# Two state-space layers: which states' drives GpSimd forms, and when ScalarE ends the sigmoid of u

## The chip, the cores and the metric

The kernel runs on one NeuronCore of a Trainium2 chip. The metric is device time in microseconds (us): the median of three executions is 6466.08 us (6462.25 to 6472.54). The engines are called PE (TensorE, the matmuls), PEld (its weight loads), DVE (VectorE), ACT (ScalarE), POOL (GpSimd) and SP (SyncE, which issues the DMAs). Each engine works through its own queue in order and waits on semaphores for the others.

## What is computed

The input `x` is (4, 128, 64, 64). Two state-space (Mamba) layers come first, then a layer that picks top blocks and one of attention at three scales. Only the first two are touched. For each of 256 sequences of 128 steps, with 128 inner channels and 16 states:

```python
u  = silu(causal_conv4(u) + conv_b)
dt = softplus(x_dbl[..., :DT_RANK] @ W_dt.T + b_dt)
def step(h, inp):                       # one time step, 16 states a channel
    u_t, dt_t, B_t, C_t = inp
    h = exp(dt_t[:, :, None] * A) * h + (dt_t * u_t)[:, :, None] * B_t[:, None, :]
    y = einsum('bds,bs->bd', h, C_t)
...
y = (y + u * Dp) * silu(z);  return y @ W_out.T
```

`exp(dt*A)` is called the decay, `dt*u*B` the drive.

## The kernel before, in words

`mamba_layer` runs twice. Its work is cut into 32 chunks of 8 sequences, so that every operand is 128 channels x 1024 (8 sequences x 128 steps). A chunk has 16 units, one for each state s. A unit is:

- the drive: for 11 states PE spreads row B over the partitions into PSUM (`pe_rows`, L441, "rows"), and DVE multiplies it by `dtu` there (`dve_drive`, L563). For the five states of `POOL_UNITS` a DMA brings the row of B, broadcast, and POOL multiplies it by `dtu` (`pool_drive`, L611). PE and DVE have no drive in such a unit.
- the decay: ACT's Exp (L533), into a `decay` buffer, or, for a state of `POOL_UNITS`, into the PSUM pair `b_ps[s % 2]` that PE does not fill in that unit.
- the scan on DVE (L577), which writes `state[s % 4]` and waits for PE's sum of state s-4.
- POOL's product of the state with row C (L617), and PE's sum of it into `y_ps` (L453, "sum"), which runs three units behind (`LAG`).

Beside that, each unit s carries a step of the preparation of the next chunk (`*_prep`), at a fixed place in each queue. What matters here:

- PE in unit s issues: rows of s (none for a state of `POOL_UNITS`), the sum of s-3, then its step of the preparation. The steps are: unit 0 the transposes ("turn", L402), units 1 and 2 the products with `w_u` (L412), unit 5 `w_bc` (L419), unit 7 `w_dt` (L425), unit 10 `w_z` (L430), unit 14 the output product of the chunk before (L465). The sum of state 0, in unit 3, has `diag` (L450, two matmuls on `u`) ahead of it, which waits for the gate.
- DVE in unit s issues: drive of s, then the gate `yz` in unit 2 (L582, waits for the sum of state 15), or its step of the preparation (u in unit 4, L542; bc in 6; the lost part in 10; z in 13) or the add in 15, then the scan of s.
- POOL in unit s issues: product of s-1, its step of the preparation (units 11, 12, 13: L594, L598, L604, the last one makes `dtu`), then the drive of s+2 if that is a state of `POOL_UNITS`.
- ACT in unit s issues: the decay of s, then its step of the preparation. The sigmoid of u is Exp (L479), Ln (L482) and Exp (L485).
- SP loads row C of s once the product of s-4 is done, then row B of s+2 if POOL forms that drive.

Below, "s4", "D4", "d4" and "p4" are the scan, DVE's drive, POOL's drive and POOL's product of state 4; a prime marks those of the neighbouring chunk. "Sum13" is PE's sum of state 13, "rows4" PE's rows for D4.

Of the kernel before, what the change touches and what calls it, by code (L numbers as in the profile page):

```python
# [27 lines left out]
def wait(eng, sem, value):  # L28

    if isinstance(value, int) and value <= 0:  # L30
        return
    eng.wait_ge(sem, value)
# [250 lines left out]
C_AT = 2 * BLOCK  # L283
GATE_AT, OUT_AT, ADD_AT = 2, 14, 15
LOAD_AT, C_WRITE_AT = 8, 11
POOL_UNITS = (2, 4, 6, 8, 10)
DVE_UNITS = tuple(s for s in range(S) if s not in POOL_UNITS)
B_ROWS, DRIVE_AHEAD, B_LOAD_AHEAD = 5, 2, 2


def mamba_layer(nc, sem, tag, X, C, M, scale_c, bias_c):
# [3 lines left out]
    with Memory(nc, tag) as m:  # L295
# [67 lines left out]
        def by_pool(c, s):  # L363

            return c * len(POOL_UNITS) + sum(1 for k in POOL_UNITS if k <= s)

        def b_slot(s):
            return POOL_UNITS.index(s)

# [63 lines left out]
        def pe_rows(pe, c, par, s):  # L433
            unit = c * S + s
            if s == 0:
                wait(pe, s_lo, c + 1)
            if s in POOL_UNITS:
                return
# [31 lines left out]
        def act_prep(act, n, par, k):  # L470
            if k == 1:
                wait(act, s_turn, n + 1)
                wait(act, s_pz, 2 * n)
                nc.scalar.activation(xt[:, :], prep_ps[:, 0:HALF], ACT.Identity, scale=scale_c[:, bass.ds(n, 1)],
                                     bias=bias_c[:, bass.ds(n, 1)]).then_inc(s_xt, 1)
            if k == 3:
                wait(act, s_pu, 2 * n + 2)
                wait(act, s_log1p, n)
                nc.scalar.activation(gu[:, :], prep_ps[:, :], ACT.Exp, scale=-1.0,  # L479
                                     bias=M["neg_conv_b"][:, 0:1]).then_inc(s_gu, 1)  # L480
                wait(act, s_gu, 3 * n + 1)
                nc.scalar.activation(gu[:, :], gu[:, :], ACT.Ln, bias=1.0).then_inc(s_gu, 1)  # L482
            if k == 4:
                wait(act, s_gu, 3 * n + 2)
                nc.scalar.activation(gu[:, :], gu[:, :], ACT.Exp, scale=-1.0).then_inc(s_gu, 1)  # L485
            if k == 5:
                wait(act, s_pbc, n + 1)
                wait(act, s_b, len(DVE_UNITS) * (n - 1))
                nc.scalar.activation(bc[:, par, :], prep_ps[:, :], ACT.Copy).then_inc(s_hi, 1)
                wait(act, s_cw, 16 * n)  # L490
                nc.scalar.activation(c_out[C_AT:C_AT + BLOCK, :], prep_ps[C_AT:C_AT + BLOCK, :],
                                     ACT.Copy).then_inc(s_cc, 1)
            if k == 8:
                wait(act, s_pdt, n + 1)
                wait(act, s_dtu, n - 1)
                wait(act, s_decay, S * (n - 1))
                nc.scalar.activation(dt[:, par, :], prep_ps[:, :], ACT.Relu, bias=M["b_dt"][:, 0:1]).then_inc(s_pos, 1)
                wait(act, s_pos, n + 1)
                nc.scalar.activation(prep_ps[:, :], prep_ps[:, :], ACT.Abs, bias=M["b_dt"][:, 0:1]).then_inc(s_abs, 1)
                wait(act, s_abs, 2 * n + 1)  # L500
                nc.scalar.activation(prep_ps[:, :], prep_ps[:, :], ACT.Exp, scale=-1.0).then_inc(s_abs, 1)
            if k == 9:
                wait(act, s_abs, 2 * n + 2)
                nc.scalar.activation(ln_e[:, :], prep_ps[:, :], ACT.Ln, bias=1.0).then_inc(s_ln, 1)
                wait(act, s_u, n + 1)
                nc.scalar.activation(gu[:, :], prep_ps[:, :], ACT.Identity, bias=1.0).then_inc(s_one, 1)
            if k == 11:
                wait(act, s_pz, 2 * n + 2)
                wait(act, s_sz, n)
                nc.scalar.activation(gz[:, :], prep_ps[:, :], ACT.Exp, scale=-1.0).then_inc(s_gz, 1)  # L510
                wait(act, s_gz, 3 * n + 1)
                nc.scalar.activation(gz[:, :], gz[:, :], ACT.Ln, bias=1.0).then_inc(s_gz, 1)
            if k == 12:
                wait(act, s_gz, 3 * n + 2)
                nc.scalar.activation(gz[:, :], gz[:, :], ACT.Exp, scale=-1.0).then_inc(s_gz, 1)

        def act_unit(act, c, par, s):
# [7 lines left out]
            seq = lambda a: by_t(a)[:, :, 1:T]  # L525
            if s in POOL_UNITS:
                wait(act, s_scan, unit + 1 - PAIRS)
# [29 lines left out]
        def dve_drive(dve, c, par, s):  # L557
            if s in POOL_UNITS:
                return
            if s == 0:  # L560
                wait(dve, s_dtu, c + 1)
            wait(dve, s_b, by_dve(c, s))
            nc.vector.tensor_tensor(b_ps[s % PAIRS][:, :], dtu[:, par, :], b_ps[s % PAIRS][:, :],  # L563
                                    ALU.mult).then_inc(s_drive, 1)
# [84 lines left out]
        def act_both(act, c, par, s, prep):  # L649
            act_unit(act, c, par, s)  # L650
            if prep:
                act_prep(act, c + 1, 1 - par, s)
# [35 lines left out]
        with nc.Block() as block:  # L688
# [24 lines left out]
            @block.scalar  # L713
            def _(act):
                act.preload_act_table_set(EXP_LN_TABLES)
                for k in range(S):
                    act_prep(act, 0, 0, k)
                run(act, act_both)
# [971 lines left out]
```

## Time and profile before

| | us |
|---|---|
| median of three executions | 6466.08 |
| the profiled execution | 6468.96 |
| its span, first to last instruction | 6467.1 |
| span of the two state-space layers (about) | 79 to 1937 and 2000 to 3857 |

The profile names, for each instruction or group of them, start, duration, engine, line, tiles out<-in and, in square brackets, how long its engine sat idle before it and who ended that. Durations of neighbours on one engine overlap a little, since a successor starts while the predecessor drains; so distances from start to start are used where an engine is busy. PEclk is the clock granted to TensorE as a share of full speed.

### The profile page before, as it was taken

The numbers are of one execution on the slowest core, as the hardware profiler recorded it, in microseconds if no ns is written. First come the engines' busy times: TensorE is split into PE (matmuls) and PEld (weight loads), VectorE is DVE, ScalarE is ACT, GpSimd is POOL, SyncE is SP. The second block draws the span as 40 slices with busy tenths as digits, with TensorE's granted clock in tenths as the row PEclk, the third lists the DMA queues.
The fourth block names the chain that finished last, engine by engine and source line by source line (L and its number), as shares of the span: only waits on it lengthen the run. The fifth ranks groups of instructions, "written<-read, shape, count | busy, mean of one in ns | idle before, by whom it ended". The sixth has DMA issues, their size and how long they took to land. (4 is left out here: it accounts for less than half of the span.)

```text
span 6467.1 us, 77508 instructions
## 1 busy us (share of the span) xinstructions
PE 5083.2 (79%) x22442; PEld 2639.5 (41%) x22442; DVE 4970.1 (77%) x6243; ACT 3277.4 (51%) x3626; POOL 4744.4 (73%) x2140
## 2 busy tenths in 40 slices
PE   3888888888874888888888866852559899898980
PEld 1343333333332333333333335311336566566650
DVE  5999999999996999999999984016465665655548
ACT  3555555555543555555555530001447677677760
POOL 3999999999994999999999970000337677676760
PEclk9999999999997999999999995875879999999995
DMA  3555555555552555555555540861569999999991
GB/s 124 202 198 201 199 200 203 203 202 199 203 176 97 200 202 205 202 200 200 200 199 204 203 147 22 343 239 27 97 123 186 179 173 186 164 185 185 184 185 52
DMA packets 1414964, 1148.54 MB, mean 178 GB/s; under 512 B 1211624, under 2 KB 1216832, under 8 KB 1406656
## 3 DMA queue, kind: packets, MB, share of 16 engines
q1 hardware_dynamic: 1414850, 1147.21, 62.3%
q8 instruction: 48, 0.79, 0.0%
q14 instruction: 66, 0.54, 0.0%
HBM read 812.29 MB, written 20.68 MB: 129 GB/s over the span
## 5 line engine op out<-in xcount | busy, mean ns | idle before, releaser
L617 POOL TENSOR_TENSOR l_state<-l_state,l_c_row 128x1024 f32<-128x1024 f32 x1024 | 2404.3, 2366 | 72.6 <-DVE l_state L577 69.0
L1389 POOL TENSOR_TENSOR l3s_el<-l3s_s_sb,l3s_eh 128x1024 f16<-128x1024 f32 (+2 forms) x584 | 1168.5, 2011 | 1217.1 <-ACT l3s_s_sb L1374 1205.7
L453 PE MATMUL l_y_ps<-l_state,ident 128*128 128x512 f32 x4096 | 1987.8, 611 | 49.0 <-POOL l_state L617 48.2
L577 DVE TENSOR_TENSOR_SCAN l_state<-l_decay,l_b_ps 128x1024 f32<-128x1024 f32 x704 | 1608.7, 2285 | 74.8 <-ACT l_decay L533 3.4
L1397 DVE TENSOR_SCALAR_CACHE_REDUCE l3s_s_sb<-l3s_s_ps 128x512 f32<-128x512 f32 (+1 forms) x1096 | 753.8, 689 | 621.9 <-PE l3s_s_ps L1333 603.2
L453 PEld LDWEIGHTS l_y_ps<-l_state,ident 128*128 128x128 f32 x4096 | 781.5, 195 | 870.2 <-issue 676.6
L1346 PE MATMUL l3s_o_ps<-l3s_vt,l3s_et 128*128 128x257 f16 x4368 | 879.5, 279 | 191.0 <-DMA l3s_et<-l3s_el 125.1
L1373 ACT ACTIVATE l3s_eh<-l3s_s_sb,l3s_shift 128x1024 f16<-128x1024 f32 (+2 forms) x584 | 634.5, 1087 | 535.4 <-DMA l3s_et<-l3s_el 423.0
L563 DVE TENSOR_TENSOR l_b_ps<-l_dtu,l_b_ps 128x1024 f32<-128x1024 f32 x704 | 850.4, 1208 | 30.2 <-PE l_b_ps L441 28.4
L441 PE MATMUL l_b_ps<-l_bc,mamba_pick 128*128 128x512 f32 x1408 | 575.1, 491 | 295.5 <-DVE l_state L577 285.6
L1348 PE MATMUL l3s_o_ps<-l3s_vt,l3s_et 128*128 128x129 f16 x4368 | 788.6, 224 | 0.0
L611 POOL TENSOR_TENSOR l_b_row<-l_b_row,l_dtu 128x1024 f32<-128x1024 f32 x320 | 756.2, 2363 | 0.2
L577 DVE TENSOR_TENSOR_SCAN l_state<-l_b_ps,l_b_row 128x1024 f32<-128x1024 f32 x320 | 729.4, 2279 | 5.1 <-POOL l_b_row L611 3.2
L1374 ACT ACTIVATE l3s_s_sb<-l3s_s_sb,l3s_shift 128x1024 f32<-128x1024 f32 (+2 forms) x584 | 629.8, 1078 | 0.0
L1346 PEld LDWEIGHTS l3s_o_ps<-l3s_vt,l3s_et 128*128 128x128 f16 x4368 | 435.0, 100 | 436.4 <-issue 204.6
L441 PEld LDWEIGHTS l_b_ps<-l_bc,mamba_pick 128*128 128x128 f32 x1408 | 230.6, 198 | 761.3 <-DVE l_state L577 583.8
L1331 PE MATMUL l3s_s_ps<-l3s_xh 128*128 128x512 f16 (+1 forms) x1096 | 426.9, 389 | 91.1 <-DVE l3s_xl L1310 69.4
L1348 PEld LDWEIGHTS l3s_o_ps<-l3s_vt,l3s_et 128*128 128x128 f16 x4368 | 435.3, 100 | 111.3 <-issue 6.6
L533 ACT ACTIVATE l_decay<-l_dt,l0m_A 128x1016 f32<-128x1016 f32 x352 | 393.0, 1134 | 141.2 <-POOL l_dt L598 99.1
L533 ACT ACTIVATE l_decay<-l_dt,l1m_A 128x1016 f32<-128x1016 f32 x352 | 393.0, 1134 | 140.4 <-POOL l_dt L598 99.6
L1332 PE MATMUL l3s_s_ps<-l3s_xl,l3s_xh 128*128 128x512 f16 (+1 forms) x1096 | 426.1, 389 | 0.0
L1333 PE MATMUL l3s_s_ps<-l3s_xh,l3s_xl 128*128 128x512 f16 (+1 forms) x1096 | 425.2, 388 | 0.0
(335 smaller groups left out, 5428.1 us busy)
## 6 DMA issues: line engine op xcount, KB each, us to landing
l_c_row<-l_c_rows SPq DMA_DIRECT2D x1024, 512.0 KB, 3.9
l_b_row<-l_c_rows SPq DMA_DIRECT2D x320, 512.0 KB, 4.9
l_ring_a<-in_L_conv_W SPq DMA_DIRECT2D x28, 1024.0 KB, 11.1
l2b_ring_b<-in_L_conv_W SPq DMA_DIRECT2D x26, 1024.0 KB, 11.3
l_xs<-X SPq DMA_DIRECT2D x64, 256.0 KB, 5.3
l_ring_a<-in_L_conv_W SPq DMA_DIRECT2D x14, 704.0 KB, 12.7
l2b_ring_b<-in_L_conv_W SPq DMA_DIRECT2D x13, 704.0 KB, 12.7
l_ring_a<-in_L_conv_W SPq DMA_DIRECT2D x14, 640.0 KB, 12.1
```

Of the source, the lines that this page charges most:

```text
L441: last = nc.tensor.matmul(b_ps[s % PAIRS][:, half(h)], C["pick"][:, s * P:(s + 1) * P], bc[:, par, half(h)], start=True, stop=True)
L453: last = nc.tensor.matmul(y_ps[:, half(h)], C["ident"][:, :], state[:, s % STATES, half(h)], start=False, stop=(s == S - 1))
L533: nc.scalar.activation(seq(to), seq(dt[:, par, :]), ACT.Exp, scale=M["A"][:, s:s + 1]).then_inc(s_decay, 1)
L563: nc.vector.tensor_tensor(b_ps[s % PAIRS][:, :], dtu[:, par, :], b_ps[s % PAIRS][:, :], ALU.mult).then_inc(s_drive, 1)
L577: nc.vector.tensor_tensor_scan(state[:, s % STATES, :], by, add, 0.0, ALU.mult, ALU.add).then_inc(s_scan, 1)
L611: nc.gpsimd.tensor_tensor(row, row, dtu[:, par, :], ALU.mult).then_inc(s_bdrive, 1)
L617: nc.gpsimd.tensor_tensor(state[:, s % STATES, :], state[:, s % STATES, :], c_row[:, s % C_ROWS, :], ALU.mult).then_inc(s_hc, 1)
L1346: high = lambda stop: nc.tensor.matmul(o_ps[par][:, 0:2 * P + 1], et[:, 0, slot, j, :], vt[:, mt, 0:2 * P + 1], start=(mt == 0), stop=stop)
L1348: lows = lambda: nc.tensor.matmul(o_ps[par][:, P:2 * P + 1], et[:, 1, slot, j, :], vt[:, mt, P:2 * P + 1], start=False, stop=False)
L1373: nc.scalar.activation(eh[:, part, off:off + EXPW], src, ACT.Exp, bias=shift[:, par:par + 1]).then_inc(s_eh, 1)
L1389: nc.gpsimd.tensor_tensor(el[:, part, off:off + EXPW], s_sb[:, par, j * EXPW:(j + 1) * EXPW], eh[:, part, off:off + EXPW], ALU.subtract).t ...
L1397: nc.vector.tensor_scalar(s_sb[:, par, kb * W:(kb + 1) * W], s_ps[(par * NB + kb) % SLOTS][:, 0:W], 0.0, None, ALU.add, ALU.max, accum_out ...
```

## The change

```diff
-POOL_UNITS = (2, 4, 6, 8, 10)
+POOL_UNITS = (3, 5, 7, 9, 11)
@@ act_prep
                 wait(act, s_gu, 3 * n + 1)
                 nc.scalar.activation(gu[:, :], gu[:, :], ACT.Ln, bias=1.0).then_inc(s_gu, 1)
-            if k == 4:
                 wait(act, s_gu, 3 * n + 2)
                 nc.scalar.activation(gu[:, :], gu[:, :], ACT.Exp, scale=-1.0).then_inc(s_gu, 1)
```

The number of drives on each engine stays at 11 and 5. PE and DVE get rows and drives in units 2, 4, 6, 8 and 10, and lose those of 3, 5, 7, 9 and 11. POOL's drives move one unit later (they are now issued in units 1, 3, 5, 7 and 9), and with them SP's loads of row B. ACT's decays of the odd states 3 to 11 go to PSUM, those of the even ones to the `decay` buffers. The third function for u is issued in unit 3, behind the Ln, and so ahead of the decay of state 4.

## Rows read from the trace of the kernel before

**Rows 1.** The page's part 1: busy us (share of the span) xinstructions.
```profile
PE 5083.2 (79%) x22442; PEld 2639.5 (41%) x22442; DVE 4970.1 (77%) x6243; ACT 3277.4 (51%) x3626; POOL 4744.4 (73%) x2140
```

**Rows 2.** Busy time in one window, 30 chunks of layer 0: span, engines, PEclk, DMA.
```profile
182.00:1882.00 1700.00, 1477.85 (x4129) 667.18 (x4128) 1644.74 (x990) 944.51 (x1049) 1670.87 (x720) 0.97 0.58 201
```

**Rows 3.** The gate L582 in windows of layers 0 and 1, then its waits in each.
```profile
L582 DVE TENSOR_TENSOR l_yz<-l_sz,l_y_ps x31: 1195/1195/1222, 182.2 to 1882.1; 128x1024 f32<-128x1024 f32 x31
...
  PE l_y_ps L453: 6.2, 6
...
L582 DVE TENSOR_TENSOR l_yz<-l_sz,l_y_ps x31: 1194/1195/1222, 2100.5 to 3801.4; 128x1024 f32<-128x1024 f32 x31
```

**Rows 4.** Waits of all DVE drives, L563: released by whom, us, times.
```profile
  PE l_b_ps L441: 28.4, 37
```

**Rows 5.** Timeline of DVE: start, duration, line, tiles; two stretches of layer 0.
```profile
1025.35 2.28 DVE L577 TENSOR_TENSOR_SCAN l_state<-l_decay,l_b_ps 128x1024 f32<-128x1024 f32 x1
...
1072.10 1.21 DVE L563 TENSOR_TENSOR l_b_ps<-l_dtu,l_b_ps 128x1024 f32<-128x1024 f32 x1
1073.22 1.21 DVE L555 TENSOR_TENSOR l_sz<-l_prep_ps,l_gz 128x1024 f32<-128x1024 f32 x1
...
1091.02 1.20 DVE L582 TENSOR_TENSOR l_yz<-l_sz,l_y_ps 128x1024 f32<-128x1024 f32 x1
1092.13 2.28 DVE L577 TENSOR_TENSOR_SCAN l_state<-l_b_ps,l_b_row 128x1024 f32<-128x1024 f32 x1
1094.33 1.21 DVE L563 TENSOR_TENSOR l_b_ps<-l_dtu,l_b_ps 128x1024 f32<-128x1024 f32 x1
1095.67 2.29 DVE L577 TENSOR_TENSOR_SCAN l_state<-l_decay,l_b_ps 128x1024 f32<-128x1024 f32 x1
1097.88 1.26 DVE L542 SCALAR_TENSOR_TENSOR l_u<-l_prep_ps,l0m_conv_b,l_gu 128x1024 f32<-128x1024 f32 x1
1099.05 2.28 DVE L577 TENSOR_TENSOR_SCAN l_state<-l_b_ps,l_b_row 128x1024 f32<-128x1024 f32 x1
```

**Rows 6.** Timeline of POOL: p15 after a wait; p13 and p14; d2; d4.
```profile
1027.70 2.36 POOL L617 TENSOR_TENSOR l_state<-l_state,l_c_row 128x1024 f32<-128x1024 f32 x1 [1.33 <-DVE l_state L577]
...
1078.82 4.67 POOL L617 TENSOR_TENSOR l_state<-l_state,l_c_row 128x1024 f32<-128x1024 f32 x2
...
1086.61 2.36 POOL L611 TENSOR_TENSOR l_b_row<-l_b_row,l_dtu 128x1024 f32<-128x1024 f32 x1
...
1093.57 2.37 POOL L611 TENSOR_TENSOR l_b_row<-l_b_row,l_dtu 128x1024 f32<-128x1024 f32 x1
```

**Rows 7.** Timeline of PE from sum13 to the first sum of the next chunk.
```profile
1081.24 1.98 PE L453 MATMUL l_y_ps<-l_state,ident 128*128 128x512 f32 x4 [0.28 <-POOL l_state L617]
1083.06 0.60 PE L402 MATMUL l_prep_ps<-ident,l_xs 128*128 128x128 f32 x4
1084.13 0.73 PE L441 MATMUL l_b_ps<-l_bc,mamba_pick 128*128 128x512 f32 x2 [0.47 <-DVE l_state L577]
1084.70 1.88 PE L453 MATMUL l_y_ps<-l_state,ident 128*128 128x512 f32 x4
1086.51 1.98 PE L412 MATMUL l_prep_ps<-l_xt,l0m_w_u 64*128 64x512 f32 x8
1088.42 1.98 PE L453 MATMUL l_y_ps<-l_state,ident 128*128 128x512 f32 x4
1090.34 1.95 PE L412 MATMUL l_prep_ps<-l_xt,l0m_w_u 64*128 64x504 f32 x8
1092.22 0.73 PE L441 MATMUL l_b_ps<-l_bc,mamba_pick 128*128 128x512 f32 x2
1092.79 1.88 PE L450 MATMUL l_y_ps<-l_u,l0m_diag_Dp 128*128 128x512 f32 x4
1094.51 3.60 PE L453 MATMUL l_y_ps<-l_state,ident 128*128 128x512 f32 x8
```

**Rows 8.** One window at the lower clock, inside sum13; columns as in rows 2.
```profile
342.70:346.10 3.40, 3.35 (x4) 1.24 (x5) 3.40 (x3) 0.00 (x0) 3.28 (x2) 0.54 0.41 164
```

## The prediction, made before the kernel was run

> **What bounds the kernel now.** The page comes first, for a summary only: no engine is busy over 80% of the whole [rows 1], since several stages with different limits are mixed there. The window over 30 chunks of layer 0 is what counts: in 1700 us DVE is busy 1645 and POOL 1671 [rows 2]. Both are nearly full, so a chunk can only get shorter if both get less to do or stand still less. The period of a chunk is read from the gate, once in each: (1882.1 - 182.2) / 30 = 56.66 us in layer 0 and (3801.4 - 2100.5) / 30 = 56.70 in layer 1 [rows 3], 56.68 in the mean.
>
> The timelines give the parts. A POOL operation takes 2.32 us from start to start: d2 to d4 has three in 6.96 [rows 6]. POOL has 16 products, 5 drives and 3 steps of preparation, 24 x 2.32 = 55.7. On DVE a scan is followed after 2.20 (1092.13 to 1094.33); a drive with its own scan right behind it, which reads what it wrote, keeps it off for 1.34 (1094.33 to 1095.67), but a drive with something else behind it only 1.12 (1072.10 to 1073.22) [rows 5]. Before, DVE's floor is 16 x 2.20 = 35.2, nine drives ahead of their scan 12.1, the drives of 13 and 15 with something between 2.2, and the six other operations (gate 1.11, u 1.17, z, bc, lost part, add) about 6.4: 55.9. So DVE sets the period, and the 0.8 above its floor is mostly waits for PE: 37 waits of drives for rows, 28.4 us in all [rows 4], and waits of the gate for the sum of state 15 [rows 3]. POOL stands still once in a chunk, for s15 [rows 6]. PE has slack, but see where: from sum13, which waits for p13 [rows 7], to rows3 it is busy almost without a hole, and rows3 at 1092.22 is done (0.73) 1.4 us before D3 at 1094.33 wants it [rows 5, 7].
>
> **The change, part by part.** (a) DVE's drives 2, 4, 6 and 10 now have the gate, u, bc and the lost part between them and their scan. Four times 1.34 - 1.12 = 0.22 makes 0.9 less: DVE's floor becomes 55.0. I take the row's value; the bound on the other side is zero. The Trainium skill (VectorE: DVE Perf Modes, "The DRAIN you can't avoid") says that in a chain of DVE operations the semaphore after each costs nothing extra; by that the floor would stay at 55.9. The two distances 1.34 and 1.12 for the same operation speak against it.
>
> (b) D11 goes, which had w_z of unit 10 right ahead of its rows. D12 has a scan more in front of it, but sum8 too. From the start of the lost part: PE takes w_z (about 1.06 at full clock), sum8 1.7, rows12 0.8, against s10, s11 and D12's turn at 5.5. It may wait by 0 to 0.4; what hides it is the slack found below.
>
> (c) POOL's order changes at the seam of the chunks. Before it was p15, d2, p0, p1, d4, p2: d2 filled the time until s0 was done. Now it is p15, p0, d3, p1, p2, d5, p3, p4. Products come earlier in POOL's queue than they did, and fewer operations lie between p4 and the next p13: p4, d7, p5, p6, d9, p7, p8, d11, p9, p10, L594, p11, L598, p12, L604, that is 15 before p13.
>
> (d) PE's order changes too, and this is what I expect to decide. rows2 now stands between w_u of unit 1 and sum15, and rows4 stands behind diag and sum0, where rows3 had stood ahead of both. The chain, by starts [rows 7]: sum13 to turn 1.82; turn 0.55 (it lasts 0.60, the overlap of neighbours is 0.05 to 0.1; its 0.47 of waiting for s15 should go, as DVE has more slack); rows1 0.57; sum14 1.81; w_u 1.91; rows2 0.57; sum15 1.92; w_u 1.88; diag 1.72; sum0 1.72; rows4 0.73 and 0.07 for the handover: 15.27 from sum13's start to D4. Then DVE: D4 to u 1.12, u to s4 1.17 [rows 5], s4's start to p4 2.35 (1025.35 to 1027.70) [rows 5, 6]. Then POOL: 15 x 2.32 = 34.8 to the next p13, and p13's start to sum13 2.42 (1078.82 to 1081.24) [rows 6, 7]. This is a closed circle through PE, DVE and POOL, and no queue can go around it faster: 15.27 + 4.64 + 34.80 + 2.42 = 57.13 us.
>
> A second circle goes through the gate. Sum13 to sum15's start 7.23, sum15 to the gate 2.05 (its duration 1.98 and the handover), gate to s2 1.11, s2 to p2 2.35, then 18 operations to p13, 41.76, and 2.42: 56.92. The same two circles before the change: through rows3 and D3, 11.26 + 1.34 + 2.35 + 16 x 2.32 + 2.42 = 54.5; through the gate 6.66 + 2.05 + 1.11 + 2.35 + 17 x 2.32 + 2.42 = 54.0. Both lay below DVE's 55.9, so they cost nothing. The change makes the first 2.6 longer: a rows, diag and sum0 more on PE (4.0), u on DVE (1.0), one POOL operation less (2.3).
>
> With 57.1 against DVE's 55.0 and POOL's 55.7 the other edits cost nothing: DVE has 2.1 us of slack a chunk, which covers (b), and POOL stands still 1.4 at p2 and p4. D4 is where DVE waits.
>
> (e) ACT's third function for u: its input, w_u of unit 2, starts 6.1 us before D4 (the last four links) and so 7.2 before u, and lasts 1.95. ACT's mean operation is 944.5 / 1049 = 0.9 us [rows 2]; I take 1.1 each for the three functions, which makes 5.3 of the 7.2, and 6.4 if decay 4 stands between them, as it did. u waits for neither. Decay 4, now behind them, ends at 6.4, and s4 starts at 8.4. Zero. Decay 3 has to wait for s1 and is then ahead of these functions; s1 is done before w_u is. Zero.
>
> (f) SP: the first load of row B now waits behind the load of row C that p13 releases, and d3 wants it three operations after it (p14, p15, p0), 7 us; before, d2 had four (L604, p13, p14, p15) behind p12. No row of mine has the landing; if it were late, POOL's idle time at p2 would take the first microsecond. I take zero, and up to 1 us a chunk as the bound above. The last chunk of each layer has no preparation; its tail goes from d11 through s11 to p15 where it went from d10: about 1 us more for each.
>
> (g) The clock. In one chunk sum13 fell into a stretch at about the lower of the two levels, 1.2 GHz: PEclk is 0.54, and the four matmuls of a sum fill 3.35 us [rows 8] where sum13 elsewhere has 1.98 and hands over after 1.82 [rows 7]. PE had stood still just before. Before, such a slow stretch near sum13 shows as a wait of the gate, in layer 0 in five periods of 30 besides the one at the start of the window (6 in the row) [rows 3], and DVE's slack there took half of it. On the new circle all of it counts. Taken at that rate: 5/30 x 1.6 = 0.3 a chunk. Bounds: zero, if PE keeps its clock; and the rate of the other weak place, where PE stands still before w_z, 37 in 62 [rows 4]: 1.0.
>
> **The sum.** The period becomes 57.13 + 0.3 = 57.4, which is 0.75 over 56.68; 62 periods make 47, and the two tails 2: +49 us. The span 6467.1 of the profiled execution (6468.96) becomes 6516; its time lies 3 above the median 6466.1, so I forecast 6515. A measurement of this kernel can tell about 0.2%, 13 us, from no change.
>
> **The rivals.** (1) The circle closes but the clock falls as often as before w_z: 57.13 + 1.0, times 62, +90, 6556. For it: PE now stands still about 2.3 us ahead of sum13, since sum12 is done early and p13 comes late. Against it: a slow stretch ahead of sum12 fills just that hole. The Trainium skill (TensorE: Matmul & The Clock Gate, "What's actually happening") has the throttled state as the default and activity as what lifts it; by that, more standing still on PE would speak for this rival. Chance 0.2.
>
> (2) Not slower but faster: the circle is not tight, because one of its links is shorter than I read (PE reaches sum13 without p13 as the last thing, or D4's rows are ready in time), by more than 1 us. Then POOL's 24 operations decide, the period is 55.7 to 55.8, 0.9 under 56.68, and the time is 6466 - 57 = 6409. For it: DVE's and PE's idle times all go, which is what (a) and (b) do locally. Against it: the links are read at full clock from one chunk, and two circles, not one, lie above 56.68. It decides from a point where the circle is under 56.6. By the skill's sentence in (a) the floor of DVE would then be 55.9 and the gain only 45. Chance 0.14.
>
> (3) No change that can be told: the circle is 0.3 to 0.5 shorter than I make it (turn, handover and the 15 POOL steps each have some hundredths) and the clock costs little: 56.7 to 56.9, within 13 us of 6466. Chance 0.14.
>
> That the change doesn't do what it says can be set aside: five drives stay on POOL either way, and the line of ACT moves within its queue.
>
> The forecast itself has 0.52; its own range is 57.0 to 57.8, 6486 to 6535. The range that should hold 8 in 10 takes in rivals 1 and 3 and leaves out most of 2: 6450 to 6575. Faster by over 0.2%: 0.15. Within it: 0.14. Slower: 0.71.
>
> **What would show it.** In the changed kernel the gate's period in both layers is 57.1 or more. DVE's drives wait for rows of PE once in nearly every chunk, at D4, by 0.5 or more, and the gate waits for the sum of state 15 in most chunks; nearly no wait in units 11 and 12. POOL stands still at p2 and p4, for scans, and no more at p15. sum13 starts 0.06 after p13 ends in nearly all chunks, with PE idle before it. What would make it wrong: rows4 done before DVE is at D4, a POOL without idle time, or DVE busy over 99% of the window.

## The result and the profile after

The changed kernel takes 6513.33 us (median of 6, 6510.67 to 6515.88) against 6466.52 for the kernel before, run beside it: a ratio of 1.0073, with a 95% interval of 1.006 to 1.0086. It is 47 us slower; 49 were forecast, 6515. In the profiled execution the span is 6511.7 us. Lines behind L484 are one lower than before.

The page's part 1 [rows 1]:

```profile
PE 5115.6 (79%) x22442; PEld 2628.2 (40%) x22442; DVE 4961.9 (76%) x6243; ACT 3276.4 (50%) x3626; POOL 4742.5 (73%) x2140
```

The same work, then, as shares of a longer span. The gate in windows of layers 0 and 1 gives the period [rows 3], and one window over 30 chunks of layer 0 the busy times [rows 2]:

```profile
L581 DVE TENSOR_TENSOR l_yz<-l_sz,l_y_ps x32: 1210/1221/1223, 182.4 to 1959.7; 128x1024 f32<-128x1024 f32 x32
...
L581 DVE TENSOR_TENSOR l_yz<-l_sz,l_y_ps x31: 1207/1220/1222, 2132.1 to 3853.1; 128x1024 f32<-128x1024 f32 x31
```

```profile
182.40:1907.90 1725.50, 1488.16 (x4128) 659.07 (x4128) 1640.17 (x991) 943.80 (x1049) 1671.12 (x721) 0.97 0.58 198
```

Layer 0 has 30 periods in the window of 1725.5 us, 57.52 each; layer 1 has (3853.1 - 2132.1) / 30 = 57.37. The mean is 57.44 against 56.68, and 60 x 0.76 = 46 us is the whole loss. DVE and POOL are as busy as they were, to a few us, and have 25 us more in which to stand still.

What DVE waited for, over both layers (us, times): first the drives L562 for rows (28.4 us in 37 waits before [rows 4]), then the gate L581 for the sum of state 15 (21.8 us in 15 waits before).

```profile
  PE l_b_ps L441: 108.9, 141
```

```profile
  PE l_y_ps L453: 33.6, 52
```

The waits for rows grew by 80 us and those of the gate by 12. The drives that no longer have their own scan right behind them gave back about 0.7 a chunk, some 45 us. The difference is the loss. Counted in DVE's timelines over 62 chunks, only 22 us of the waits for rows are D4's (58 times); 27 are D2's (40 times), 33 are D1's (21 times) and 24 are D15's (18 times). D11's, which were nearly all of the 28 before, are gone.

The seam between two chunks in the timelines. DVE [rows 5]:

```profile
1044.02 2.29 DVE L576 TENSOR_TENSOR_SCAN l_state<-l_decay,l_b_ps 128x1024 f32<-128x1024 f32 x1
1046.99 1.23 DVE L562 TENSOR_TENSOR l_b_ps<-l_dtu,l_b_ps 128x1024 f32<-128x1024 f32 x1 [0.68 <-PE l_b_ps L441]
1048.70 1.22 DVE L581 TENSOR_TENSOR l_yz<-l_sz,l_y_ps 128x1024 f32<-128x1024 f32 x1 [0.49 <-PE l_y_ps L453]
1049.84 2.28 DVE L576 TENSOR_TENSOR_SCAN l_state<-l_decay,l_b_ps 128x1024 f32<-128x1024 f32 x1
1052.04 2.27 DVE L576 TENSOR_TENSOR_SCAN l_state<-l_b_ps,l_b_row 128x1024 f32<-128x1024 f32 x1
1054.68 1.23 DVE L562 TENSOR_TENSOR l_b_ps<-l_dtu,l_b_ps 128x1024 f32<-128x1024 f32 x1 [0.37 <-PE l_b_ps L441]
1055.82 1.28 DVE L541 SCALAR_TENSOR_TENSOR l_u<-l_prep_ps,l0m_conv_b,l_gu 128x1024 f32<-128x1024 f32 x1
1057.01 2.28 DVE L576 TENSOR_TENSOR_SCAN l_state<-l_decay,l_b_ps 128x1024 f32<-128x1024 f32 x1
```

POOL: p13 to p0 in one row, then d3, p1, and p2 and p4 each after a wait [rows 6]:

```profile
1037.37 9.29 POOL L616 TENSOR_TENSOR l_state<-l_state,l_c_row 128x1024 f32<-128x1024 f32 x4
...
1052.20 2.38 POOL L616 TENSOR_TENSOR l_state<-l_state,l_c_row 128x1024 f32<-128x1024 f32 x1 [0.92 <-DVE l_state L576]
...
1059.45 2.36 POOL L616 TENSOR_TENSOR l_state<-l_state,l_c_row 128x1024 f32<-128x1024 f32 x1 [0.24 <-DVE l_state L576]
```

PE, from sum13 to rows4, and the next sum13 [rows 7]:

```profile
1039.76 1.99 PE L453 MATMUL l_y_ps<-l_state,ident 128*128 128x512 f32 x4 [2.16 <-POOL l_state L616]
1041.59 0.60 PE L402 MATMUL l_prep_ps<-ident,l_xs 128*128 128x128 f32 x4
1041.94 0.71 PE L441 MATMUL l_b_ps<-l_bc,mamba_pick 128*128 128x512 f32 x2
1042.49 1.88 PE L453 MATMUL l_y_ps<-l_state,ident 128*128 128x512 f32 x4
1044.30 1.98 PE L412 MATMUL l_prep_ps<-l_xt,l0m_w_u 64*128 64x512 f32 x8
1046.21 0.74 PE L441 MATMUL l_b_ps<-l_bc,mamba_pick 128*128 128x512 f32 x2
1046.79 1.88 PE L453 MATMUL l_y_ps<-l_state,ident 128*128 128x512 f32 x4
1048.60 1.95 PE L412 MATMUL l_prep_ps<-l_xt,l0m_w_u 64*128 64x504 f32 x8
1050.48 1.98 PE L450 MATMUL l_y_ps<-l_u,l0m_diag_Dp 128*128 128x512 f32 x4
1052.30 1.88 PE L453 MATMUL l_y_ps<-l_state,ident 128*128 128x512 f32 x4
1053.62 1.02 PE L441 MATMUL l_b_ps<-l_bc,mamba_pick 128*128 128x512 f32 x2
...
1096.65 1.98 PE L453 MATMUL l_y_ps<-l_state,ident 128*128 128x512 f32 x4 [1.23 <-POOL l_state L616]
```

Read in this order: PE stands still 2.16 us for p13, then has not one hole until rows4 at 1053.62. rows4 ends at 1054.64, and D4 starts at 1054.68 after 0.37 of waiting. s4 follows at 1057.01, p4 at 1059.45 after a wait for it, POOL then runs without a hole to the next p13, and sum13 comes 56.89 us after the last. That is the circle, each link with its wait at the right place.

In other chunks sum13 ran at the lower clock, and took 3.50 us from its start to the next matmul where the chunk above has 1.83. PE's timeline and a window on it (PEclk 0.51; columns as in rows 2) [rows 8]:

```profile
462.62 3.67 PE L453 MATMUL l_y_ps<-l_state,ident 128*128 128x512 f32 x4 [2.17 <-POOL l_state L616]
...
466.12 0.60 PE L402 MATMUL l_prep_ps<-ident,l_xs 128*128 128x128 f32 x4
```

```profile
462.60:466.10 3.50, 3.48 (x4) 1.41 (x5) 2.90 (x2) 0.00 (x0) 3.50 (x2) 0.51 0.68 254
```

Of the 60 periods 36 are between 55.5 and 57.3 us, most of them 56.8 or 57.0; 20 are 58.4 to 58.7, and 4 are near 57.7. In the 20 it is sum13 that ran at the lower clock. In the 4 it is the output product (L465) and the sum of state 11 ahead of it (PEclk 0.59 from 1314.90 to 1320.60): PE now stands still 2.2 us ahead of that sum as well, in 58 of 59 chunks, where in the kernel before it did so in none:

```profile
1314.87 2.75 PE L453 MATMUL l_y_ps<-l_state,ident 128*128 128x512 f32 x4 [2.18 <-POOL l_state L616]
1317.41 3.51 PE L465 MATMUL l_prep_ps<-l0m_w_out,l_yz 128*128 128x64 f32 x16
```

D15, whose rows stand behind them, then waits 2.2 us.

### The profile page after: what moved, and what is told of

The parts are those of the page before. It is cut to its first block and busy times, and to the rows that moved or that the text cites. A ratio compares the mean times of both kernels' runs of the same rounds, so it can differ in the third digit from the quotient of the medians.

```text
span 6511.7 us, 77620 instructions
## 1 busy us (share of the span) xinstructions
PE 5115.6 (79%) x22442; PEld 2628.2 (40%) x22442; DVE 4961.9 (76%) x6243; ACT 3276.4 (50%) x3626; POOL 4742.5 (73%) x2140
## 5 line engine op out<-in xcount | busy, mean ns | idle before, releaser
L453 PE MATMUL l_y_ps<-l_state,ident 128*128 128x512 f32 x4096 | 2056.4, 630 | 367.2 <-POOL l_state L616 365.8
L453 PEld LDWEIGHTS l_y_ps<-l_state,ident 128*128 128x128 f32 x4096 | 754.1, 195 | 1278.5 <-issue 625.7
L562 DVE TENSOR_TENSOR l_b_ps<-l_dtu,l_b_ps 128x1024 f32<-128x1024 f32 x704 | 853.1, 1212 | 111.0 <-PE l_b_ps L441 108.9
L441 PE MATMUL l_b_ps<-l_bc,mamba_pick 128*128 128x512 f32 x1408 | 620.3, 522 | 90.5 <-DVE l_state L576 90.3
L441 PEld LDWEIGHTS l_b_ps<-l_bc,mamba_pick 128*128 128x128 f32 x1408 | 245.4, 193 | 436.2 <-DVE l_state L576 250.2
```

The lines of the kernel that those rows point to most:

```text
L441: last = nc.tensor.matmul(b_ps[s % PAIRS][:, half(h)], C["pick"][:, s * P:(s + 1) * P], bc[:, par, half(h)], start=True, stop=True)
L453: last = nc.tensor.matmul(y_ps[:, half(h)], C["ident"][:, :], state[:, s % STATES, half(h)], start=False, stop=(s == S - 1))
```

## The experiments

All ratios are to the kernel before, run beside it on the same chip; a bracket is the 95% interval.

### The two edits apart

```diff
 e1_act_only:  only the line "if k == 4:" of act_prep taken out
 e2_units_only: only POOL_UNITS = (3, 5, 7, 9, 11)
```

> The kernel before with only the edit on ScalarE: the third function for u follows the second at once. Theory (the loss comes from PE's circle through sum13, rows2, rows4, D4): no change, 6466 within 5 us, the gate's period stays 56.7. Rival (the moved function holds up decay 4, or u is what was late): 6440 or less, or 6480 or more.

> The changed kernel with the edit on ScalarE undone: only the states of GpSimd's drives are changed. Theory: as the changed kernel, 6513 within 8 us; u is formed at the same place, as its third function ends 1 to 2 us before DVE is there. Rival (the two edits belong together, u would be late without the second): over 6530.

The first took 6468.5 us, 0.9999 [0.9989, 1.0008]; the second 6519.4, 1.0077 [1.006, 1.0095]. The edit on ScalarE is worth nothing that can be told, alone or on top of the other. All of the loss is in the choice of the states.

### Which states: the units 0 to 4 put back, or only unit 2

```diff
 e3_seam_kept:
-POOL_UNITS = (3, 5, 7, 9, 11)
+POOL_UNITS = (2, 4, 7, 9, 11)
 e7_unit2_back:
+POOL_UNITS = (2, 5, 7, 9, 11)
```

> The changed kernel with POOL_UNITS = (2, 4, 7, 9, 11): the units 0 to 4 are as before, the later ones as changed. Theory (only the order at the seam, rows2 and rows4 in PE's chain, costs): the circle is back at 54.5, DVE has two of the four shorter drives (floor 55.5), no wait of D11 behind w_z, POOL's 24 operations bound it at 55.7; with the gate's waits in slow stretches 56.0 to 56.2, that is 6425 to 6440. Rival (POOL's drives being a unit later is what costs, three of five still are): 6485 to 6500.

> The changed kernel with POOL_UNITS = (2, 5, 7, 9, 11): D2 and rows2 are gone again and d2 fills POOL's hole at the seam, but D3 and rows3 are there and rows4 stays behind diag and sum0. Theory, main circle (through rows4 and D4): its length is unchanged, rows3 takes the place of rows2, period 56.9 at full clock, 57.4 in the mean, 6505 to 6520; the gate's circle gets 0.6 shorter, so no waits of the gate at full clock. Rival (the gate's circle with rows2, or POOL's hole before p0 and p2, is what costs): 6440 to 6470.

Both were misses: 6548.7 us, 1.0122 [1.0105, 1.0139], and 6547.8, 1.0119 [1.0102, 1.0136]. Both are slower than the changed kernel. With (2, 4, 7, 9, 11) the links rows2 and rows4 are gone from PE, and the period is longer still, (1922.4 - 184.5) / 30 = 57.93. POOL's timeline of that kernel, p3 to p6:

```profile
1003.94 2.37 POOL L616 TENSOR_TENSOR l_state<-l_state,l_c_row 128x1024 f32<-128x1024 f32 x1 [1.16 <-DVE l_state L576]
1007.41 2.36 POOL L616 TENSOR_TENSOR l_state<-l_state,l_c_row 128x1024 f32<-128x1024 f32 x1 [1.10 <-DVE l_state L576]
1009.72 2.36 POOL L610 TENSOR_TENSOR l_b_row<-l_b_row,l_dtu 128x1024 f32<-128x1024 f32 x1
1012.04 2.35 POOL L616 TENSOR_TENSOR l_state<-l_state,l_c_row 128x1024 f32<-128x1024 f32 x1
1015.54 2.37 POOL L616 TENSOR_TENSOR l_state<-l_state,l_c_row 128x1024 f32<-128x1024 f32 x1 [1.15 <-DVE l_state L576]
```

POOL waits for s3 before p3, for s4 before p4 and for s6 before p6. So there is a circle that I had not added up. It goes from sum13 to the gate, on through DVE's queue all the way to s6, then to p6, and from there through POOL. Its links, by starts in that kernel's timelines: on PE turn, rows1, sum14, w_u, sum15 and the gate, 1.82 + 0.36 + 0.55 + 1.81 + 1.91 + 2.05 = 8.5. On DVE gate to s2 1.11, D3 2.2, s3 1.34, u 2.2, s4 1.18, D5 2.2, s5 1.33, D6 2.2, bc 1.24, s6 1.24, and s6 to p6 2.35: 18.6. On POOL from p6 twelve operations (p6, d9, p7, p8, d11, p9, p10, L593, p11, L597, p12, L603) of 2.32 to p13: 27.8. And 2.4 to sum13. That makes 57.3; the full-clock periods of that kernel are 57.3 to 57.6. Another 20 of its 60 periods are 59.0 to 59.2, with sum13 at the lower clock. The gate, from which this circle enters DVE's queue, waits for PE in 26 of 31 chunks of layer 0:

```profile
  PE l_y_ps L453: 44.2, 26
```

The second kernel, (2, 5, 7, 9, 11), is explained in the same way with p4, for which its POOL waits 1.15 us:

```profile
1009.14 2.37 POOL L616 TENSOR_TENSOR l_state<-l_state,l_c_row 128x1024 f32<-128x1024 f32 x1 [1.15 <-DVE l_state L576]
```

The gate to s2 is 1.11, then D3 2.2, s3 1.34, D4 2.2, u 1.12, s4 1.17 and p4 2.35, 11.5 on DVE. With 8.5 on PE, 15 POOL operations or 34.8, and 2.4, that is 57.2, where its full-clock periods are 57.2 to 57.6 (24 of 60 are slower, 58.9 to 59.1). Its unit 3 has a drive on DVE again, which lengthens this circle; I had overlooked that, since I compared only the circles that the changed kernel has. These sums were made after the runs; the links are measured, but no further run was made that changes one of these two circles alone.

What follows, as far as these sums go: it is the circle p13, sum13, PE's chain, DVE, p(k), POOL that counts, as predicted, but every k has to be tried. A drive that POOL gives up early in the chunk is one that DVE must do between the gate and p(k), and one that POOL takes up late lies between p(k) and p13.

### The same cut in PE's chain, in both kernels

```diff
-                for back in (2 * k - 2, 2 * k - 1):
+                for back in (0,) if k == 1 else (2, 3):
```

> The changed kernel without one of the four taps of the convolution (two of the four products with w_u of unit 1 are left out, so u is another): PE's work between sum14 and rows2 is 0.95 us shorter, nothing is taken from DVE or POOL. Theory (a circle from sum13 through PE to D4 sets the period): 0.95 less at full clock, until the 55.8 of POOL's 24 operations bound it; 56.9 becomes 55.9, with slow stretches 56.3, so 57.4 - 56.3 = 1.1 a chunk, 6445 to 6465. Rival (DVE's or POOL's order costs by itself, PE is not in it): 6505 or more.

> The kernel before without the same tap. Theory: PE has 1.4 us of slack there at full clock, so only the gate's waits in slow stretches go (about 13 us in both layers together): 6450 to 6463. Rival (PE's work at the seam always counted): 6410 or less.

One tap of the convolution is left out, so u and all behind it differ. In the changed kernel this gave 6467.0 us, 1.0000 [0.9991, 1.001], that is 0.73% less than the change alone. In the kernel before it gave 6446.6, 0.9967 [0.9956, 0.9979], 0.33% less. Neither is in its expected range: the first by 2 us, the second by 3. The mean period falls from 57.44 to 56.53, close to the 0.95 that was taken out. The full-clock period falls from 56.9 to 55.8, POOL's floor, in 20 of the 60 periods. In 26 it is 56.6: there the sum of state 11 ran at the lower clock and D15 waits 1.1 us for its rows. In 12, with sum13 at the lower clock, it is 57.4 to 57.8. The kernel before got 21 us, where I had allowed the gate's 13: the gate's waits fell from 21.8 to 10.3 us and those of the drives from 28.4 to 23.3, which is 17 of the 21. Part of it is at the start of the layers, which have the same product in their way: the first gate of layer 0 comes 1.9 us sooner. So the cut is worth over twice as much after the change as before it. PE's chain was at the edge before and is on the path after. The product left out stands ahead of sum15 too, so this run cuts both circles of the prediction; so do the next two sections. That the one through D4 closes last is read from the trace: p4 waits for s4 in 56 of the 60 periods, 0.2 us each, which it would not if the gate's circle were the longer.

### POOL's part of the circle

```diff
-            if k == 13:
+            if k == 14:
                 wait(pool, s_dt, n + 1)
```

> The changed kernel with GpSimd's last step of preparation (L603, dtu) moved from unit 13 to unit 14, that is behind p13 in place of ahead of it. The work is the same. Theory (the circle runs through POOL's queue up to p13 and from there through PE): sum13 can start 2.3 us earlier, then p14 and sum14 come last and give 0.4 of that back to the path as a gain: full-clock period 56.45 for 56.87, 6482 to 6495. Rival (the order of POOL before p13 is not on the path): 6508 or more; slower if DVE's first drive now waits for dtu.

6471.6 us, 1.0004 [0.9994, 1.0014]: back to the kernel before, 10 us better than expected. Nothing is left out; one POOL operation stands behind p13 and not ahead of it. Most periods are 56.2 to 56.8, as expected (56.45). No period is over 58 in this profile, since sum13 never ran at the lower clock. There are 11 of 57.3 to 57.7; in these it is again the sum of state 11 and the output product that ran at the lower clock (PEclk 0.51 from 1185 to 1192), and D15 waits 1.9 to 2.2 us. D0 now waits for dtu in half of the chunks, but their periods, 56.2 to 56.7, are no longer than the others (L603 is the new dtu):

```profile
  POOL l_dtu L603: 22.9, 33
```

### PE's hole before sum13

```diff
 e9_turn_first (e10_turn_first_x4 also has "for j in 4 * tuple(range(CHUNK_N // 2))")
+            if prep and s == 0:
+                pe_prep(pe, c + 1, 1 - par, s)
             late = behind(c, par, s, LAG)
             if late:
                 pe_sum(pe, *late)
-            if prep:
+            if prep and s > 0:
                 pe_prep(pe, c + 1, 1 - par, s)
```

> The changed kernel with the transposes of unit 0 issued ahead of sum13 and four times over (same data each time): they fill PE's hole of 2.2 us before sum13, and the 0.35 of the transposes leaves the circle. Theory: full-clock period 56.9 - 0.35 = 56.5; if the hole is what lets the clock fall on sum13, the 20 periods of 60 that take 58.5 vanish and the mean is 56.5 to 56.7: 6455 to 6472. Rival (the clock falls whatever PE does there): the slow periods stay, 57.1, 6485 to 6495. Rival (the circle does not hold): over 6510.

> The changed kernel with the transposes of unit 0 ahead of sum13, once and not four times over. Theory: the full-clock period is 56.5, as with four; but PE's hole before sum13 stays 1.8 us, so the slow periods of 58 us, which four times over removed, stay in good part: 6485 to 6500, against 6482 there. Rival (the slow periods went for another reason, the place of the transposes): 6483 or less.

Four times over took 6482.6 us, 1.0024 [1.0014, 1.0033]; once took 6471.8, 1.0007 [0.9998, 1.0017]. Most periods are 56.3 to 56.7 with one and 56.5 to 56.9 with four, against 56.9 in the changed kernel: about the 0.35 of the transposes, which were on the circle. Beyond that both expectations fail: the time with four is 10 us over its range, and with one it is where the rival put it (6483 or less). With four, 3 of 60 periods are over 58; with one, PE still stands still 1.75 us before sum13 in half of the chunks, and none is over 58. In the 12 of 57.3 to 57.8, and in the 3 with four, it was the sum of state 11 and the output product that ran at the lower clock, and not sum13. So the hole ahead of sum13 need not be filled. Moving the transposes into it, or, in the run above, moving p13 forward, was enough to keep sum13 at the full clock: there is no longer one hole of 2.2 us right ahead of it. The mean period is the same 56.73 with one and with four. That four times over is still 11 us slower comes from outside the loop: the first gate of layer 0 comes 2.9 us later (185.1 for 182.3), the way from the last gate of layer 0 to the first of layer 1 takes 3.9 more, and the last chunk of layer 1 takes 2.0 more. At the start of the layers the transposes stand alone and take 3.7 us for 1.0 to 1.1.

### Searching for a better kernel

In the kernel before, most of DVE's waits for rows are those of D11, which stand behind w_z. They can be taken away there:

```diff
 pe_unit of the kernel before (e11_rows11_ahead)
-            pe_rows(pe, c, par, s)
+            if s != 11:
+                pe_rows(pe, c, par, s)
             late = behind(c, par, s, LAG)
             if late:
                 pe_sum(pe, *late)
+            if s == 10:
+                pe_rows(pe, c, par, 11)
```

> The kernel before with the two rows matmuls of state 11 issued at the end of unit 10's sum, ahead of w_z: D11 no longer waits for PE behind w_z. Theory (before, DVE sets the period and its 28.4 us of waits for rows add to it): most of the 28 us goes, 6435 to 6448, bounded by POOL's 24 x 2.32 = 55.7 a chunk. Rival (other waits take their place, POOL or the gate): 6460 or more.

6449.4 us, 0.9974 [0.9963, 0.9986]: 18 us faster than the kernel before and some 64 faster than the changed one (not run side by side), the best of all that compute the whole. No drive waits for rows any more, where 37 did [rows 4]. It is just short of the expected range, since part of the gain is given back at the gate, whose waits grow from 21.8 to 33.4 us:

```profile
  PE l_y_ps L453: 33.4, 25
```

Then the transposes were put ahead of sum13, four times over, in this kernel and in one that avoids w_z by another choice of states:

```diff
 e12_rows11_turn_x4: e11_rows11_ahead, and as e13_unit11_turn_x4 below, the first line excepted
 e13_unit11_turn_x4: the kernel before with
-POOL_UNITS = (2, 4, 6, 8, 10)
+POOL_UNITS = (2, 4, 6, 8, 11)
-                for j in range(CHUNK_N // 2):
+                for j in 4 * tuple(range(CHUNK_N // 2)):
+            if prep and s == 0:
+                pe_prep(pe, c + 1, 1 - par, s)
...
-            if prep:
+            if prep and s > 0:
```

> The kernel before with the rows of state 11 ahead of w_z and the transposes ahead of sum13, four times over. Theory: after the first edit alone the only waits left in DVE were the gate's, 0.9 us in about half of the periods, when sum13 ran at the lower clock; PE's hole there being filled, they go, and the period is DVE's floor of 55.92 throughout: 6420 to 6435. Rival (the lower clock moves elsewhere and costs the same there): 6445 or more.

> The kernel before with POOL_UNITS = (2, 4, 6, 8, 11) and the transposes ahead of sum13, four times over. Here I use circles through the gate and on to every product p(k), not only p2 and p4: the longest is through D10, the lost part, s10 and p10, 56.0 less 0.35 for the transposes, 55.6; DVE's floor falls by 0.2 to 55.7, POOL's 24 operations stand at 55.75. So 55.8 a chunk: 6415 to 6430, and no more wait behind w_z. Rival (circles are no guide, what counts is how many of POOL's drives come late): 6470 or more, as with (2, 4, 7, 9, 11).

Both went wrong: 6540.8 us, 1.011 [1.0093, 1.0127], and 6509.3, 1.0064 [1.0048, 1.0081]. The timelines of the first, DVE's add and gate with PE's transposes between them:

```profile
1038.10 0.68 DVE L586 TENSOR_TENSOR X<-X,l_prep_ps 128x512 f32 x1
...
1048.63 1.22 DVE L582 TENSOR_TENSOR l_yz<-l_sz,l_y_ps 128x1024 f32<-128x1024 f32 x1 [0.63 <-PE l_y_ps L453]
```

```profile
1037.12 0.73 PE L441 MATMUL l_b_ps<-l_bc,mamba_pick 128*128 128x512 f32 x2 [1.09 <-DVE l_state L577]
1038.92 1.94 PE L402 MATMUL l_prep_ps<-ident,l_xs 128*128 128x128 f32 x16 [1.07 <-DVE X L586]
1040.70 1.88 PE L453 MATMUL l_y_ps<-l_state,ident 128*128 128x512 f32 x4
```

The transposes write the PSUM tile that the add reads, so they can't start before the add of unit 15 has ended. In the changed kernel DVE is there early and this costs nothing. In the kernel before DVE has no slack, and from its add a new circle goes through transposes (1.78), sum13, rows1, sum14, w_u and sum15 to the gate: 1048.63 - 1038.10 = 10.53 us, where DVE's own work between the two takes 9.8. The period is 55.92 + 0.7 = 56.65 at full clock, and 58.3 in 43 of 60 chunks: right after the wait of 1.07 us the transposes or sum13 run at the lower clock. In the second kernel DVE goes from its add at 1031.41 to its gate at 1041.94, 10.53 us again with 0.63 of waiting, and the gate waits in 31 of the 32 chunks of layer 0. But its usual period is 57.4 and not 56.65, since w_z isn't avoided either. The rows of D12 now stand behind it and sum8, and D12 waits in 50 of 62 chunks, 44 us in all:

```profile
1018.75 1.23 DVE L563 TENSOR_TENSOR l_b_ps<-l_dtu,l_b_ps 128x1024 f32<-128x1024 f32 x1 [0.87 <-PE l_b_ps L441]
```

So a wait that cost nothing where DVE had slack became the path where it had none. Whether (2, 4, 6, 8, 11) is good without the moved transposes wasn't tried.

## Why the prediction was right, point by point

- **What bounds the kernel.** Right: DVE before, a circle over three engines after. The tap left out moves the one over twice as much as the other.
- **(a) the shorter drives.** Right for three of four: D4 keeps DVE off for 1.14, D10 for 1.12, and D2 for 1.11 to 1.12 in the few chunks in which the gate doesn't wait. Behind D6, bc starts only after 1.23 to 1.25, so that one gives 0.1. The sentence of the Trainium skill cited there (VectorE: DVE Perf Modes, "The DRAIN you can't avoid"), that a semaphore in a chain of DVE operations costs nothing extra, doesn't describe these rows: 1.34 and 1.14 for the same drive in the same kernel. It was worth no time here, since DVE was no longer the bound.
- **(b) D11, D12.** Right: neither unit has a wait for rows left.
- **(c), (d) the circle.** Forecast 57.13 us at full clock, measured 56.89 in the chunk shown. By links: PE from sum13 to D4 14.92 for 15.27 (the transposes hand over after 0.35 and not 0.55; rows4 starts 1.32 after sum0 and not 1.72, but lasts 1.02 and not 0.73), DVE 4.77 for 4.64 (p4 starts 2.44 after s4 and not 2.35), POOL and the handover 37.20 for 37.22. The other circle showed too: the gate waits in 52 places where it did in 15. D4 waits in 58 of 62 chunks as forecast, but by 0.38 in the mean and not 0.5 or more, and the waits of D15, D1 and D2, which are most of the 109 us, were not foreseen. POOL stands still at p2 and p4, and hardly at p15, as forecast.
- **(e) the ScalarE edit.** Zero, shown by both runs.
- **(f) SP.** d3 ran right behind p0 without a wait; no wait for the row B loads shows.
- **(g) the clock.** This term was too small: 0.3 us a chunk forecast, 57.44 - 56.87 = 0.57 measured, where 56.87 is the distance between two sum13 in undisturbed chunks. A third of the chunks lose 1.7 us, where the rate taken was a sixth. The reason given was right, that nothing absorbs it any more, but the rate rose as well, some way towards rival 1. What was said against that rival showed too: in 14 of 58 chunks the sum of state 11, or the output product behind it, ran at the lower clock, and only 1.2 us of the hole ahead of sum13 were left; sum13 ran at the full clock in all of them.
- **The sum.** The circle was forecast 0.25 too long and the clock 0.27 too small; that 57.4 was met to 0.05 is partly luck. Either alone would have stayed inside the range.
- **The rivals.** The faster one is out: the full-clock period is 56.9, and the one period under 56, 55.5, is that of a last chunk, which has no preparation. No change is out by the interval. Rival 1 came true in part.
- **What the prediction did not see** is how general its own circle is. Applied only to p2 and p4 it gave the right number for this change, and the wrong sign for the next one, (2, 4, 7, 9, 11).

## What to carry to other kernels

When two engines are both nearly full (DVE 97% and POOL 98% here) with work that is handed around, add up every closed path through the queues: out of one queue, through the others and back one iteration later, for every hand-over point and not only for those near the edit. An edit that shortens an engine's own work can lengthen such a path. Here it did so on a helper engine (PE, 86% busy) that has a long stretch without a hole. Such a sum is only a lower bound: (2, 4, 6, 8, 11) was forecast with every p(k) tried, and still missed a circle that the moved transposes had made, and rows behind w_z. A wait that is free where the engine has slack is not free in a variant in which it has none.

## What the runs showed of the hardware

- In the changed kernel sum13 ran at the lower clock in 20 of 58 chunks and then handed over after 2.9 to 3.5 us for 1.8 (PEclk 0.51 in one such window). All 20 are among the 40 in which PE had stood still 2.2 us right before; in the 14 in which it had stood still 1.2 us there was none. But 20 of those 40 kept the full clock, and in the kernel before it fell in 10 of 23 chunks with holes of 1.1 and 0.6 to 0.8 us around rows0. With 1.75 us or less ahead of sum13 in the kernels with moved transposes or a moved dtu, sum13 ran at the full clock in all chunks. What exactly of the holes matters, length or place, the runs leave open.
- On DVE a drive followed by the partial (32-partition) step bc keeps it off for 1.23 to 1.25 us, where two full operations without dependence take 1.11 to 1.14. The runs don't show why.
